# A two-layer convolution kernel on one core: a shorter transform step and an earlier input load in layer 0, and another order of the steps in layer 1

## The chip, the core and the metric

The kernel runs on one core of a Trainium2 chip. The core has five engines that work side by side, each through its own list of instructions in order: TensorE (PE, matrix products, its weight loads are listed as PEld), VectorE (DVE), ScalarE (ACT), GpSimd (POOL) and SyncE (SP), which here only issues DMA transfers. Engines wait for each other by semaphores. The metric is the device time of the whole program in microseconds (us), the median of several runs.

## The reference

The input `x` is 4 images of 64 channels, 256 by 256, in float32. Two layers follow each other, each on its group-normalised input, and each adds its result to its input:

```python
hidden = einsum('bchw,oc->bohw', x, w_hidden) + b_hidden          # 64 -> 384 channels
hidden = depthwise 3x3 convolution of hidden + b_dw
q, k, v = split(hidden, 3)                                        # 128 channels each
out = irfft2(rfft2(patches8x8(q)) * rfft2(patches8x8(k)))         # per 8x8 patch
out = layernorm over the channels of out * ln_w + ln_b
layer 0:  x = x + einsum('bchw,oc->bohw', v * out, w_proj) + b_proj

kern = w_span @ relu(batchnorm(w_reduce @ x)) + b_span            # 9 numbers per pixel
z = softplus(sum over the 9 taps of kern[tap] * x shifted by tap) # involution
layer 1:  x = x + softplus(conv3x3(z, w_conv2) + b_conv2)
```

## The kernel before, in words

**Stages.** A setup block makes the weights. A second block takes the statistics of the first image. Then comes layer 0, a short block that takes layer 1's statistics, and layer 1. Both layers walk over strips of 8 image rows: 128 strips in layer 0, 132 in layer 1 (the last few are padding). The order on each engine is written out by hand in functions called `body`; there is no scheduler. `run` (L411) and `run1` (L1187) call them: once plainly for the first pass and then in hardware loops.

**Layer 0.** One pass of `body` does two strips in eight steps, k = 0 to 7, four to a strip. `run` makes the plain first pass, and then, for each further image, a loop of 13 or 14 passes and a loop of one pass at the image's border, where the next image's statistics are finished (`averages` on PE, L622, while PE waits for DVE). The fourth and last long loop has 17 passes, i = 47 to 63. In a step PE makes four tiles of the q and k convolution (L550), in even steps `project` (L583, L585), in odd steps `variance` (L616, which needs the square `sq` that ACT makes at L719), the v convolution (L567), the forward transform (L606), and the inverse transform of the step before (L597, which needs `u` after POOL's subtraction of the mean, L517). ACT copies the results out of PSUM. After each forward transform `freq_copy` (L699) makes eight copies: two for `k_swap`, two for `q_im`, two for `q_re`, and two more of two partitions each (L711, L712), which put the purely real frequencies right. Once per strip ACT normalises the input, `normed` (L675, tile `xn`) in step 0, and rounds it, `high_parts` (L681) in step 1. POOL makes the low parts in step 2 (`low_parts`, L498); DVE adds up the results (`finish`, L852) and builds the stacked copies (`high_stacks`, `both_stacks`) behind it in steps 2 and 3, ahead of its product for step 3 (L818). SP loads the input (`load`, L429) for the strip after the one that was just normalised.

**Layer 1.** `body` does four strips. For a strip, PE spreads nine kernels over the channels (`select`, L1309, two banks in turn), DVE multiplies each with the shifted input (L1570, tile `prod`), and POOL adds seven of the nine products up (L1292, six additions), which DVE adds into `b_x` (L1518). ACT and DVE make the softplus and write `z` (L1528). PE convolves `z` in two halves of six products each (`conv`, L1327), DVE adds the input (`residual`, L1555), and POOL adds the logarithm (L1299) before the store. Besides, PE makes the next kernels: `r_product` (L1314) twice, ACT's relu between (L1443), then `weights` (L1319), split into three bfloat16 parts by ACT (L1451, L1456) and DVE (`rest` L1536, `third_parts` L1541), stored and read back in another layout by SP (`stack_parts`, `stack_back`). Bank 7 holds in turn the second half of the convolution, the relu's input, the kernels and the rest of the split, so these wait for each other.

Of the kernel before, what the change touches and what calls it, by code (L numbers as in the profile page):

```python
# [39 lines left out]
def build_program(nc, A, NI, S):  # L40
# [13 lines left out]
    with ExitStack() as ctx:  # L54
# [24 lines left out]
        imag_sign = sb("imag_sign", [P, 2])  # L79
        mean_w = sb("mean_w", [P, P])  # L80
# [10 lines left out]
        with ExitStack() as ph:  # L91
# [13 lines left out]
            wmax = tsb("wmax", [P, 4])  # L105
            loaded = ph.enter_context(nc.semaphore("weights_loaded"))
# [16 lines left out]
            def _(sp):  # L123
# [15 lines left out]
                sp.wait_ge(transforms_loaded, 16 * 24)  # L139
# [20 lines left out]
            def _(pool):  # L160
                for t in (bh, bdw, bd):
                    last = nc.gpsimd.memset(t[:, KQ:KV], 0.0)
# [7 lines left out]
            def _(v):  # L170
# [9 lines left out]
                v.wait_ge(v_loaded, 16 * 7)  # L180
                then(v.tensor_scalar(proj_scale[:], proj_w[:], ln_wb[:, 0:1], None, ALU.mult))
# [124 lines left out]
        with ExitStack() as ph:  # L306
# [60 lines left out]
            q_split = tsem("q_split")  # L367
# [43 lines left out]
            def run(eng, body, tail=None):  # L411
                body(0, True, NI > 1, None)
                start = 1
                for n in range(1, NI):
                    with eng.Fori(start, n * IT - 2) as i:
                        body(i, False, True, None)
                    with eng.Fori(n * IT - 2, n * IT - 1) as i:
                        body(i, False, n < NI - 1, n)
# [7 lines left out]
            def _(sp):  # L426
# [20 lines left out]
                def body(i, first, stats, image):  # L447
# [8 lines left out]
                    for b in range(2):  # L456
                        if not (first and b == 0):
                            to, of, of_res = i * 2 * R + b * R, i * 2 * R + (b + 1) * R, i * 2 * R + (b + 1) * R + 1
                            normed_before, pairs_before = i * 2 + b, i * 4 + 2 * b
                            if not first:  # L460
                                to, of, of_res = sp.snap(to), sp.snap(of), sp.snap(of_res)
                                normed_before, pairs_before = sp.snap(normed_before), sp.snap(pairs_before)

                            sp.wait_ge(xn_made, normed_before)
                            load(of, 1 - b)

# [19 lines left out]
            def _(pool):  # L486
# [33 lines left out]
                def body(i, first, stats, image):  # L520
# [21 lines left out]
            def _(pe):  # L542
# [83 lines left out]
                def body(i, first, stats, image):  # L626
                    for k in range(8):
# [5 lines left out]
                        for t in range(4):  # L633
                            if t % 2 == 0 and not (first and k == 0):
                                pe.wait_ge(qk_copied, i * 16 + (2 * k - 1 + t // 2))
                            last = conv(b, b_qk[t // 2][:, KQ * (t % 2):KQ * (t % 2) + KQ], 4 * cg + t)
                            if t % 2:
                                last.then_inc(qk_conv, 1)
# [9 lines left out]
                        def transform_ready():  # L648
                            pe.wait_ge(qk_copied, i * 16 + (2 * k + 2))
                            if not (first and k == 0):  # L650
                                pe.wait_ge(k_read, i * 8 + k)
                                pe.wait_ge(q_split, i * 8 + k)
# [15 lines left out]
            def _(act):  # L668
                def normed(s, b):
                    act.wait_ge(x_loaded[b], (s - b) * 16 + 32)  # L670
                    act.wait_ge(par_ready, s + 1)
                    if not isinstance(s, int) or s >= 1:
                        act.wait_ge(stacks_ready, s + 0)
                        act.wait_ge(hi_made, s + 0)
                    act.activation(xn[:, :, 0:SL], xr[b][:].rearrange("p s w -> p w s"), ACT.Identity, bias=par[b][:, 1:2],  # L675
                                   scale=par[b][:, 0:1]).then_inc(xn_made, 1)
# [21 lines left out]
                def freq_copy(i, k, any_before):  # L698
# [11 lines left out]
                    act.wait_ge(q_copied, i * 8 + k)  # L710
                    act.copy(by_block(q_re[C:C + 2, :]), b_q[C:C + 2])  # L711
# [1030 lines left out]
```

## Time and profile before

| what | value |
|---|---|
| median of 3 runs | 10036.34 us |
| lowest and highest | 10029.1 and 10041.79 us |
| the profiled execution's own time | 10034.93 us |
| its span, first to last instruction | 10033.1 us |
| mean granted clock of PE | 0.988 of full |
| busy: PE, DVE, ACT, POOL | 9128.4, 6036.7, 6973.9, 4896.1 us |

The profile is of one execution. The share of busy time is a mean over stages with different limits, so each stage is read by itself. Layer 0 runs from about 200 to 7110 us, layer 1 from about 7430 us to the end. In a row of the timeline, the number in square brackets is the time that the engine was idle just before, and the arrow names what ended it; "issue" means that no wait seen in the trace explains it.

### The profile page before, as it was taken

How to read it: one execution, taken by the hardware profiler on the slowest of the kernel's cores; microseconds unless marked ns; L12 is line 12 of the kernel's file. 1: busy time of each engine (PE TensorE's matmuls, PEld its weight loads, DVE VectorE, ACT ScalarE, POOL GpSimd, SP SyncE). 2: the span in 40 equal slices, each digit the busy share in tenths (PEclk: the TensorE clock that was granted, in tenths of full speed). 3: DMA queues.
4: the chain of work that ended last, by engine and by line, in shares of the span. 5: the costliest groups of instructions: out<-in, count | busy, mean ns of one | idle time of the engine just before them, and what ended most of it. 6: DMA issues, size and time to landing. Idle time of an engine off the chain costs nothing. (4 is left out here: it accounts for less than half of the span.)

```text
span 10033.1 us, 169594 instructions
## 1 busy us (share of the span) xinstructions
PE 9128.4 (91%) x58854; PEld 5045.6 (50%) x58854; DVE 6036.7 (60%) x7784; ACT 6973.9 (70%) x9573; POOL 4896.1 (49%) x2751
## 2 busy tenths in 40 slices
PE   1999999999999999999999999999868888888888
PEld 0666666666666666666665555555322222222222
DVE  4555555555555555555555454544558888888887
ACT  1777777777777777777776767767217777777777
POOL 1334433343344344433433333333118888888888
PEclk9999999999999999999999999999989999999999
DMA  6122222222222222222212111111764444444444
GB/s 129 47 60 55 48 57 56 56 50 55 60 55 47 59 56 55 50 55 60 55 39 48 39 48 39 47 40 39 162 157 105 104 104 104 104 104 104 104 104 102
DMA packets 619184, 718.26 MB, mean 72 GB/s; under 512 B 44324, under 2 KB 578138, under 8 KB 595142
## 3 DMA queue, kind: packets, MB, share of 16 engines
q1 hardware_dynamic: 618950, 714.70, 30.2%
q8 instruction: 200, 3.28, 0.1%
q14 instruction: 34, 0.28, 0.0%
HBM read 549.65 MB, written 164.89 MB: 71 GB/s over the span
## 5 line engine op out<-in xcount | busy, mean ns | idle before, releaser
L550 PE MATMUL banks<-w_hi,hi_lo 128*128 128x256 f16 x18432 | 2380.6, 275 | 132.5 <-issue 80.9
L550 PEld LDWEIGHTS banks<-w_hi,hi_lo 128*128 128x128 f16 x18432 | 1795.2, 99 | 556.4 <-issue 209.9
L508 POOL TENSOR_TENSOR u_im<-q_im,k_swap 128x512 f32<-128x512 f32 x512 | 706.4, 1380 | 2136.2 <-ACT q_im L706 2082.8
L1292 POOL TENSOR_TENSOR part_sum<-part_sum,prod 128x1024 f32<-128x1024 f32 x660 | 1559.8, 2363 | 261.7 <-DVE prod L1570 218.8
L1327 PE MATMUL banks<-z,conv_w 128*128 128x512 f32 x3140 | 1523.4, 614 | 0.0
L688 ACT ACTIVATE qk<-banks,inv_wscale 128x512 f32<-128x512 f32 x1024 | 689.9, 687 | 1040.8 <-PE banks L550 1028.4
L818 DVE TENSOR_TENSOR u<-q_re,banks 128x512 f32<-128x512 f32 x512 | 351.0, 686 | 1717.1 <-ACT q_re L712 1341.5
L511 POOL TENSOR_TENSOR u<-u,u_im 128x512 f32<-128x512 f32 x512 | 649.7, 1269 | 1338.8 <-DVE u L818 1338.8
L567 PE MATMUL banks<-hi_lo,w_hi 128*128 128x512 f16 x4608 | 1085.7, 381 | 13.9 <-DVE tmp L887 13.9
L550 PE MATMUL banks<-w_lo_pair,hi_pair 128*128 128x256 f16 x6144 | 1012.0, 274 | 0.0
L498 POOL TENSOR_TENSOR hl_all<-xn,hi_all 64x1280 f16<-64x1280 f32 x258 | 793.2, 3074 | 241.2 <-ACT hi_all L681 219.2
L1327 PEld LDWEIGHTS banks<-z,conv_w 128*128 128x128 f32 x3140 | 540.6, 188 | 613.2 <-issue 613.2
L517 POOL TENSOR_TENSOR u<-u,u_mean 128x512 f32<-128x512 f32 x512 | 532.2, 1039 | 513.4 <-DVE u_mean L833 513.4
L567 PEld LDWEIGHTS banks<-hi_lo,w_hi 128*128 128x128 f16 x4608 | 431.0, 98 | 650.5 <-issue 209.9
L597 PEld LDWEIGHTS banks<-idft,u 128*128 128x128 f32 x4096 | 496.3, 191 | 511.8 <-issue 322.7
L696 ACT ACTIVATE v_s<-banks,inv_wscale 128x512 f32<-128x512 f32 x512 | 349.6, 683 | 546.4 <-PE banks L567 546.4
L675 ACT ACTIVATE xn<-xr,par 128x2816 f32<-128x2816 f32 x129 | 684.0, 5302 | 27.0 <-DMA xr<-in_x_dram 27.0
L1570 DVE TENSOR_TENSOR prod<-banks,x_up 128x1024 f32<-128x1024 f32 x396 | 482.6, 1219 | 313.6 <-PE banks L1309 313.6
L597 PE MATMUL banks<-idft,u 128*128 128x128 f32 x4096 | 594.0, 288 | 73.8 <-POOL u L517 73.8
L550 PEld LDWEIGHTS banks<-w_lo_pair,hi_pair 128*128 128x128 f16 x6144 | 604.3, 98 | 72.6
L1309 PE MATMUL banks<-kern_parts,sel 64*128 64x512 bf16 x2380 | 443.7, 388 | 196.8 <-DVE prod L1570 196.5
L831 DVE TENSOR_REDUCE u_mean<-u 128x4 f32<-128x512 f32 x512 | 351.0, 686 | 434.0 <-POOL u L511 434.0
(210 smaller groups left out, 16400.3 us busy)
## 6 DMA issues: line engine op xcount, KB each, us to landing
xr<-in_x_dram SPq DMA_DIRECT2D x258, 640.0 KB, 9.1
xb<-y_scratch SPq DMA_DIRECT2D x268, 320.0 KB, 4.8
xa<-y_scratch SPq DMA_DIRECT2D x270, 256.0 KB, 5.3
x_res<-in_x_dram SPq DMA_DIRECT2D x258, 256.0 KB, 4.2
out_dram<-res SPq DMA_DIRECT2D x258, 256.0 KB, 5.1
y_scratch<-ys SPq DMA_DIRECT2D x256, 256.0 KB, 4.1
yc<-y_scratch SPq DMA_DIRECT2D x256, 256.0 KB, 6.0
xs<-in_x_dram SPq DMA_DIRECT2D x92, 512.0 KB, 7.1
```

Source lines behind the costliest of these rows:

```text
L498: nc.gpsimd.tensor_tensor(hl_all[C:P, 1 + c0:1 + c1, 1:SL], xn[C:P, c0:c1, 0:SL - 1], hi_all[C:P, 1 + c0:1 + c1, 0:SL - 1], ALU.subtract). ...
L508: nc.gpsimd.tensor_tensor(u_im[:], q_im[:], k_swap[:], ALU.mult).then_inc(u_made, 1)
L511: nc.gpsimd.tensor_tensor(u[:], u[:], u_im[:], ALU.add).then_inc(u_step, 1)
L517: nc.gpsimd.tensor_tensor(u4, u4, u_mean[:].unsqueeze(2).to_broadcast([P, 4, P]), ALU.subtract)\
L550: r = pe.matmul(out, px, w, start=n == 0, stop=n == 13)
L567: r = pe.matmul(b_v[:], w, px, start=n == 0, stop=n == 13)
L597: last = pe.matmul(by_patch[:, p, t], u[:, block], idft[:], start=True, stop=True)
L675: act.activation(xn[:, :, 0:SL], xr[b][:].rearrange("p s w -> p w s"), ACT.Identity, bias=par[b][:, 1:2], scale=par[b][:, 0:1]).then_inc(x ...
L688: act.activation(qk[:, 2 * h:2 * h + 2, :], b_qk[h][:].rearrange("p (t c) -> p t c", t=2), ACT.Copy, scale=inv_wscale[:, 0:1]).then_inc(qk ...
L1292: nc.gpsimd.tensor_tensor(part_sum[:], prod[0][:] if n == 0 else part_sum[:], prod[n + 1][:], ALU.add)\
L1327: last = pe.matmul(b_c[h][:], conv_w[:, n, :], z[b][:, 2 * h + j:2 * h + j + 2, dc:dc + W], start=n == 0, stop=n == 5)
L1570: v.tensor_tensor(by_row(to), by_row(flat(b_kern[(9 * k + n) % 2])), src[:, :, 1 + dc:1 + dc + W], ALU.mult).then_inc(prod_ready, 1)
```

## The change

**Layer 0.** The two small copies of `freq_copy` go, with their semaphore. In their place the setup block changes the transform's tables, so that the purely real frequencies pass through the same product as the others: the columns of `dft` become half the sum and half the difference of a pair, rows are added in `idft` (four more small loads, `idft_other`), and signs are changed. `normed` is done in two halves of the columns: the first in step 3 of the strip before, the second where the whole one stood, in step 0. SP loads a strip's input when the strip two before it has been normalised, ahead of the residual's load and the store. `averages` becomes eight small matmuls instead of one. The last pass, i = 63, has a loop of its own, so that the long last loop has 16 passes.

**Layer 1.** The same instructions stand in another order on every engine.

```diff
                     act.copy(by_block(q_re[0:C, :]), b_q[0:C])
                     act.copy(by_block(q_re[C:P, :]), b_q[0:C]).then_inc(q_copied, 1)
-                    act.wait_ge(q_copied, i * 8 + k)
-                    act.copy(by_block(q_re[C:C + 2, :]), b_q[C:C + 2])
-                    act.copy(by_block(q_re[C + 32:C + 34, :]), b_q[C + 32:C + 34]).then_inc(q_split, 1)
...
+                        if k % 4 == 3 and not (last and k == 7):
+                            normed(i * 2 + (k // 4 + 2), k // 4, 0)
                         if k % 4 == 0:
-                            normed(i * 2 + (k // 4 + 1), (k // 4 + 1) % 2)
+                            normed(i * 2 + (k // 4 + 1), (k // 4 + 1) % 2, 1)
...
                 def averages(image):
-                    pe.matmul(b_v[:, 0:2], pair_avg[:], tmp[:, 0:2, :].rearrange("p a i -> p (a i)"), start=True, stop=True)\
-                        .then_inc(gn_answered, 1)
+                    for q in range(4):
+                        for a in range(2):
+                            made = pe.matmul(b_v[32 * q:32 * q + 32, a:a + 1], pair_avg[:, 32 * q:32 * q + 32], tmp[:, a, :],
+                                             start=True, stop=True)
...
-                with eng.Fori(start, NB) as i:
-                    body(i, False, False, None)
+                with eng.Fori(start, NB - 1) as i:
+                    body(i, False, False, None, False)
+                with eng.Fori(NB - 1, NB) as i:
+                    body(i, False, False, None, True)
```

On POOL the last addition moves from the end of a strip to the start of the next:

```diff
+                        if not (first and k < 3):
+                            b = (k - 3) % 2
+                            nc.gpsimd.tensor_tensor(res[b][:], res[b][:], ab2[b][:], ALU.add).then_inc(out_ready, 1)
```

On SP, within a strip:

```diff
                         sp.wait_ge(mid_normed, normed_before)
-                        load_a(of_a, of_a1, (k + 1) % 2)
+                        load_a(of_a, of_a1, k % 2)
+                        stack_parts(made, k + 1)
                         if not (first and k < 3):
                             sp.wait_ge(out_ready, given_out)
                             store(to, (k + 1) % 2)
-                        stack_parts(made, k)
                         sp.wait_ge(parts_stored, stored)
-                        stack_back(0, (k + 2) % 4)
+                        for h in range(2):
+                            stack_back(h, (k + 1) % 4)
                         if not (first and k < 2):
                             sp.wait_ge(resid_added[1], given)
-                        stack_back(1, (k + 2) % 4)
                         load_b(of, (k + 2) % 4)
```

What stands in a row on the engines, at three places. The numbers behind `banks` are pairs of PSUM banks, those behind the other names are buffers.

ScalarE in layer 0, from the root of an odd step (step 3) into step 4, before:

```order
L726 ACTIVATE rs<-rs 128x512
L693 REGISTER_ALU
L696 ACTIVATE v_s3<-banks2,inv_wscale 128x512
L703 COPY k_swap<-banks1 64x512
L704 COPY k_swap<-banks1 64x512
L705 ACTIVATE q_im<-banks1,imag_sign 64x512
L706 ACTIVATE q_im<-banks1,imag_sign 64x512
L707 COPY q_re<-banks1 64x512
L708 COPY q_re<-banks1 64x512
L711 COPY q_re<-banks1 2x512
L712 COPY q_re<-banks1 2x512
L719 ACTIVATE sq0<-banks2 128x512
```

The same place in the changed kernel (the second half of `xn` follows two `qk` copies behind this piece):

```order
L703 ACTIVATE xn<-xr0,par0 128x128x11
L721 REGISTER_ALU
L724 ACTIVATE v_s3<-banks2,inv_wscale 128x512
L731 COPY k_swap<-banks1 64x512
L732 COPY k_swap<-banks1 64x512
L733 ACTIVATE q_im<-banks1,imag_sign 64x512
L734 ACTIVATE q_im<-banks1,imag_sign 64x512
L735 COPY q_re<-banks1 64x512
L736 COPY q_re<-banks1 64x512
L743 ACTIVATE sq0<-banks2 128x512
```

The first half of `xn` now stands before `v_s3`, and the two copies of two partitions before `sq0` are gone.

TensorE in layer 1, around the two products that make `r` (`x_mid` by `wr`), before:

```order
L1342 REGISTER_ALU
L1314 MATMUL banks3<-x_mid0,wr 128x512
L1337 REGISTER_ALU
L1309 MATMUL banks0<-kern_parts2,sel 128x512 x2
L1349 REGISTER_ALU
L1314 MATMUL banks3<-x_mid0,wr 128x512
L1337 REGISTER_ALU
L1309 MATMUL banks1<-kern_parts2,sel 128x512 x2
L1352 REGISTER_ALU
L1327 MATMUL banks3<-z1,conv_w 128x512
L1337 REGISTER_ALU
L1309 MATMUL banks0<-kern_parts2,sel 128x512 x2
```

The same in the changed kernel:

```order
L1378 REGISTER_ALU
L1340 MATMUL banks3<-x_mid0,wr 128x512
L1353 MATMUL banks3<-z1,conv_w 128x512
L1386 REGISTER_ALU
L1335 MATMUL banks1<-kern_parts3,sel 128x512 x2
L1389 REGISTER_ALU
L1340 MATMUL banks3<-x_mid0,wr 128x512
L1391 REGISTER_ALU
L1335 MATMUL banks0<-kern_parts3,sel 128x512 x2
L1353 MATMUL banks3<-z1,conv_w 128x512
L1395 REGISTER_ALU
L1345 MATMUL banks3<-rn,span_w 32x256 x4
```

The two products stood between the kernels of one strip (`kern_parts3`, or 2). Now they stand behind its last kernel, with a product of the convolution and a kernel of the next strip between them.

VectorE in layer 1, from the first product of a strip, before:

```order
L1564 REGISTER_ALU
L1568 REGISTER_ALU
L1570 TENSOR_TENSOR prod0<-banks0,x_up0 128x1024
L1573 REGISTER_ALU
L1574 REGISTER_ALU
L1518 TENSOR_TENSOR banks2<-banks2,part_sum 128x1024
L1564 REGISTER_ALU
L1570 TENSOR_TENSOR prod1<-banks1,x_up0 128x1024
L1551 REGISTER_ALU
L1553 ISA
L1554 ISA
L1555 SCALAR_TENSOR_TENSOR res0<-banks3,neg_b,xb0 128x512
```

The same in the changed kernel:

```order
L1610 TENSOR_TENSOR prod0<-banks1,x_up1 128x1024
L1602 REGISTER_ALU
L1610 TENSOR_TENSOR prod1<-banks0,x_up1 128x1024
L1556 TENSOR_TENSOR banks2<-banks2,prod8 128x1024
L1571 REGISTER_ALU
L1574 SCALAR_TENSOR_TENSOR banks3<-banks3,span_b,k_parts 128x256
L1618 REGISTER_ALU
L1619 REGISTER_ALU
L1556 TENSOR_TENSOR banks2<-banks2,part_sum 128x1024
L1579 TENSOR_TENSOR k_parts<-banks3,k_parts 128x256
```

The second product of the strip is now made first; the addition of `prod8`, which closed the strip before, comes behind it, and with it the two steps of the split (`span_b` and `k_parts`) of the next strip.

## Rows read from the trace of the kernel before

**Rows 1.** Stages: length; busy us of PE, PEld, DVE, ACT, POOL; clock; DMA:

```profile
200.00:5280.00 5080.00, 4923.42 (x38340) 3140.90 (x38340) 2768.92 (x3967) 3799.62 (x5176) 2006.56 (x1341) 1.00 0.23 54
5280.00:7110.00 1830.00, 1694.34 (x12868) 1068.10 (x12866) 891.24 (x1267) 1277.37 (x1744) 674.90 (x453) 0.97 0.18 42
...
7500.00:10033.00 2533.00, 2231.41 (x7062) 741.55 (x7060) 2074.24 (x2088) 1863.67 (x2611) 2160.08 (x915) 1.00 0.43 104
```

**Rows 2.** Waits over the whole run: us in total, times, longest us:

```profile
PE banks L616 <- ACT sq L719: 103.4, 128, 1.2
...
PE banks L550 <- issue: 80.9, 32, 3.3
...
PE banks L597 <- POOL u L517: 73.8, 127, 5.7
```

**Rows 3.** Timeline of ACT in layer 0: start us, us, what [idle before]:

```profile
3016.51 5.30 ACT L675 ACTIVATE xn<-xr,par 128x2816 f32<-128x2816 f32 x1
...
3037.34 0.58 ACT L711 COPY q_re<-banks 2x512 f32<-2x512 f32 x1
...
3057.75 0.69 ACT L696 ACTIVATE v_s<-banks,inv_wscale 128x512 f32<-128x512 f32 x1 [1.77 <-PE banks L567]
...
3069.09 5.32 ACT L675 ACTIVATE xn<-xr,par 128x2816 f32<-128x2816 f32 x1
```

**Rows 4.** Timeline of POOL and DVE in step 2 of a strip:

```profile
3042.81 2.71 POOL L498 TENSOR_TENSOR hl_all<-xn,hi_all 64x1280 f16<-64x1280 f32 x1
...
3042.99 3.52 DVE L852 TENSOR_TENSOR ys<-ys,t_n 128x512 f32<-128x512 f32 x1
```

**Rows 5.** Timeline of PE in the fourth long loop of layer 0:

```profile
5289.11 0.82 PE L550 MATMUL banks<-w_hi,hi_lo 128*128 128x256 f16 x3 [2.96 <-issue]
5291.74 1.44 PE L550 MATMUL banks<-w_hi,hi_lo 128*128 128x256 f16 x6 [1.81 <-issue]
...
5400.97 0.82 PE L550 MATMUL banks<-w_hi,hi_lo 128*128 128x256 f16 x3 [2.64 <-issue]
...
6978.48 0.82 PE L550 MATMUL banks<-w_hi,hi_lo 128*128 128x256 f16 x3 [3.27 <-issue]
```

**Rows 6.** DMA queue of instructions, 2800 to 3800 us, then 5600 to 6600 us:

```profile
q8 instruction: 13, 0.21, 0.1%
...
q8 instruction: 80, 1.31, 0.6%
```

**Rows 7.** Timeline of PE over one strip of layer 1:

```profile
8402.26 3.70 PE L1327 MATMUL banks<-z,conv_w 128*128 128x512 f32 x8
...
8409.94 0.39 PE L1309 MATMUL banks<-kern_parts,sel 64*128 64x512 bf16 x2 [1.20 <-DVE prod L1570]
8410.59 1.13 PE L1314 MATMUL banks<-x_mid,wr 128*128 128x512 f32 x2 [0.27 <-DVE res L1555]
...
8412.59 1.13 PE L1314 MATMUL banks<-x_mid,wr 128*128 128x512 f32 x2 [0.47 <-ACT rn L1443]
8413.99 0.39 PE L1309 MATMUL banks<-kern_parts,sel 64*128 64x512 bf16 x2 [0.27 <-DVE prod L1570]
8414.31 1.13 PE L1327 MATMUL banks<-z,conv_w 128*128 128x512 f32 x2
...
8421.59 3.70 PE L1327 MATMUL banks<-z,conv_w 128*128 128x512 f32 x8
```

**Rows 8.** Timeline of POOL over the same strip:

```profile
8420.34 2.36 POOL L1299 TENSOR_TENSOR res<-res,ab 128x1024 f32<-128x1024 f32 x1 [0.40 <-ACT ab L1470]
...
8427.13 12.13 POOL L1292 TENSOR_TENSOR part_sum<-part_sum,prod 128x1024 f32<-128x1024 f32 x5 [1.68 <-DVE prod L1570]
```

**Rows 9.** Page: a product on DVE (mean ns), loads to landing:

```profile
L1570 DVE TENSOR_TENSOR prod<-banks,x_up 128x1024 f32<-128x1024 f32 x396 | 482.6, 1219 | 313.6 <-PE banks L1309 313.6
...
xb<-y_scratch SPq DMA_DIRECT2D x268, 320.0 KB, 4.8
```

**Rows 10.** Timeline of the setup block: a small VectorE step, a small load's issue:

```profile
31.14 0.25 DVE L182 TENSOR_SCALAR proj_shift<-proj_w,ln_wb 128x64 f32<-128x64 f32 x1
...
14.69 0.47 SPq L134 DMA_DIRECT2D dft<-in_dft_dram  x1
```

More of the change, by code:

```diff
@@ L79, in build_program @@
         imag_sign = sb("imag_sign", [P, 2])
+        own_sign = sb("own_sign", [P, 1])
         mean_w = sb("mean_w", [P, P])
@@ L138, in _ @@
                                     .then_inc(transforms_loaded, 16)
-                sp.wait_ge(transforms_loaded, 16 * 24)
+                    sp.wait_ge(v_cleared, 1)
+                    for part in range(2):
+                        for half in range(2):
+                            lo, src = C * part + 32 * half, C * (1 - part) + 2 * half
+                            sp.dma_start(idft_other[lo:lo + 2], A["idft"][src:src + 2]).then_inc(transforms_loaded, 16)
+                sp.wait_ge(transforms_loaded, 16 * 28)
                 sp.wait_ge(turned, 16)
@@ L411, in run @@
             def run(eng, body, tail=None):
-                body(0, True, NI > 1, None)
+                body(0, True, NI > 1, None, False)
                 start = 1
@@ L445, in load_stats, with body @@
                                      A["x"][:, bass.ds(row + R * h, R), :]).then_inc(xs_loaded, 16)
-                def body(i, first, stats, image):
+                def body(i, first, stats, image, last):
                     if stats:
@@ L518, in less_mean, with body @@
                         .then_inc(u_ready, 1)
-                def body(i, first, stats, image):
+                def body(i, first, stats, image, last):
                     for k in range(8):
@@ L733, in next_root, with body @@
                     act.activation(g_root[:, 1:2], g_root[:, 0:1], ACT.Exp, scale=-0.5).then_inc(gn_answered, 1)
-                def body(i, first, stats, image):
+                def body(i, first, stats, image, last):
                     for k in range(8):
@@ L900, in next_params, with body @@
                                            src[:, 0:1, image:image + 1].to_broadcast([P, S, 1])))
-                def body(i, first, stats, image):
+                def body(i, first, stats, image, last):
                     for k in range(8):
@@ L1476, in body @@
                         u2, b2 = i * 4 + (k + 2), (k + 2) % 4
+                        v, bv = i * 4 + (k - 2), k % 2
+                        second_parts(u1)
+                        norm_up(u1, b1)
+                        if any_1:
+                            z_abs(i, k, any_2)
+                            z_exp(i, k)
+                        if any_2:
+                            conv_abs(v, bv, 0, not (first and k < 4))
+                        if any_1:
+                            z_log(i, k)
                         params(u2, b2)
@@ L1592, in _ @@
                 v.wait_ge(sel_ready, 2)
-                for u in range(2):
-                    rest(u)
-                    third_parts(u)
+                rest(0)
+                third_parts(0)
                 run1(v, body)
```

226 lines of the change are left out of this document (124 added, 102 removed).

## Prediction

> **What bounds the kernel now.** I read the stage table first [rows 1], then the waits of the whole run [rows 2], then one strip of each layer on the timeline. In the middle of layer 0 the reader is to see PE busy 4923 of 5080 us at full clock, while no other engine passes 3800: PE is the bound, and its 157 us of idle time are all that a better order can win there. The waits say who makes them: `variance` waits for ACT's square, 128 times and 103.4 us, and the inverse transform waits for POOL's `u`, 127 times and 73.8 us [rows 2]. That is one wait of each kind per strip, 1.38 us together. A third group, 80.9 us in 32 waits for "issue", has no releaser. All of it stands in the fourth long loop, where the clock is 0.97 as well [rows 1, 2]. In layer 1 a strip lasts 19.33 us [rows 7]; in 2533 us there are 131 of them, and per strip PE is busy 2231 / 131 = 17.0 us, POOL 16.5, DVE 15.8 and ACT 14.2 [rows 1]. Nobody is full: the engines hand over to each other one after another, and the order decides.
>
> **Layer 0, the two waits per strip: minus 177 us.** ACT's two copies of two partitions go, 0.58 us each [rows 3]: 1.16 per step, 4.6 per strip. Half of `xn` (2.65 of 5.3 us [rows 3]) leaves step 0 for step 3. The square that `variance` misses by about 0.81 us (103.4 / 128) is the one of step 1, behind `xn` of step 0: it now ends some 1.16 + 2.65 = 3.8 us earlier, so this wait goes. The other is `u` in step 3, missed by 0.58 us (73.8 / 127). DVE's product now waits for the first copies of `q_re` and not for the small ones, so `u` comes about 1.2 us earlier. PE, having lost its other wait, arrives 0.8 earlier too, measured from the strip's start, but so does all that feeds `u`; I lay it out with some 0.6 us to spare. It is the narrower of the two. The `finish` addition on DVE in that step still takes 3.52 us beside POOL's `low_parts` [rows 4], and the change leaves that as it was.
>
> The half of `xn` in step 3 stands before `v_s`, where ACT had 1.77 us idle [rows 3]. So `v_s` comes about 0.9 us later and the frequency copies about 0.6 us. PE wants them only in the next step, more than 3 us later, so this costs nothing; if that cover were gone it would be at most 0.9 us per strip, 115 us in all. The input load is issued a strip earlier in the queue and lands within 10 us, against 50 us until it is used: no cost. Waiting for both halves of `xn` delays the masks and `high_parts` by nothing, since the second half ends earlier than the whole did. Sum: 103.4 + 73.8 = 177 us. After that PE has no wait left in the strip, and it stands at about 52.58 - 1.4 = 51.2 us.
>
> **Layer 0, the fourth loop: minus 119 us.** At each of its 16 returns PE stands 2.96 us before the first matmul and 1.81 us before the fourth [rows 5]. The first pass starts at 5289.11 and the last at 6978.48, so a pass lasts 112.62 us, against 2 x 52.58 = 105.16 in the loops before [rows 3, 5]: 7.46 us each, of which 4.8 are standing and the rest is the lower clock after it. The instruction queue says why: 13 packets in a thousand us of the third loop, but 80 in a thousand of the fourth, nine per pass [rows 6]. A packet is 16,384 bytes (1.31 MB / 80), which holds 256 instructions of PE's compiled list, at 64 bytes each. The body has 1,656 instructions on PE, 6.5 packets. Counted in the compiled lists, the fourth loop begins about 9 instructions before the end of a packet's block, so that it touches eight blocks. The loops without a stall have 155, 192 and 229 instructions in their first block and touch seven. The change makes `averages` 28 instructions longer, three times ahead of the fourth loop, and this shifts it: the second to fourth loops now have 164, 173 and 182 in their first block, seven blocks each. I take the whole stall as gone, 16 x 7.46 = 119 us. No engine but PE has a body of more than a few blocks. The ends of this term are 0 and 119; the quiet loops are the nearest rows, so I take 119. The seven additional matmuls at each of three image borders are tiny ones in a wait for DVE that is there already: nothing.
>
> The Trainium skill ("Runtime: NRT & Kernel Launch", section "Instruction fetch mechanics") says that PE holds 2048 instructions, and also that a taken branch forces a fetch if its target lies outside a window of two pages. By the second, every return of every long loop would stall, before and after, and this term would be 0; this trace has 32 such waits in 16 of some 60 returns, so it does not agree with that rule, and it is nearer to the first.
>
> **Layer 1: minus 291 us.** A strip's four waits of PE are 1.20, 0.27, 0.47 and 0.27 us, 2.21 together [rows 7]. 19.33 - 2.21 = 17.12. The instructions are the same, so the floors stand: PE 17.0; POOL six additions of 2.43 (12.13 for five) and one of 2.36, 16.9 with hardly a gap [rows 8]. What keeps POOL from it now is a gap of 1.68 us before its second addition and 0.40 before the last [rows 8]; the order now puts the last addition at a strip's start and a product of DVE ahead of it, which fills both. I laid the new order out from these durations, with zero at a strip's first product on DVE: the old order comes to 19.2 in that layout, against 19.33. The narrow places of the new one: `third_parts` is ready at 6.2 us and PE wants bank 7 for the convolution at 6.4; the kernels' parts are back at about 13 and `select` of the next strip wants them at 16.5; `xb` lands at 20.5 (4.8 us of load [rows 9]) and is wanted at 21.4. All just hold. PE's larger number of changes between kinds of matmul (eight for seven) adds at most 0.3. I take 17.1: 131 x 2.22 = 291 us. The other ends: 16.9 by POOL (minus 26 us more), and 19.33, no gain.
>
> **Setup: plus 4.5 us.** Four loads at 0.47 us of issue and a dozen small VectorE steps at 0.25 [rows 10] make 4.9, of which a part lies beside other loads.
>
> **Sum.** 10033 - 177 - 119 - 291 + 4.5 = 9450. From start to start of the strips the first two waits come to 182 us in place of 177, since the clock and the gaps around them go too: 9446. The profiled execution took 1.8 us over its span and the median 1.4 more, so 9449 for the median.
>
> **Rivals.**
>
> *Layer 1 is held by another hand-over, at about 18 us.* Every margin above is below 1 us, and each is passed on through bank 7: relu, convolution, kernels, split. In the layout, 0.1 us more on each of ACT's instructions makes 17.7, and an `xb` that lands 3 us later makes 18.1. For it speaks that durations under load vary by such amounts (a DVE addition of 128x512 takes 3.52 us beside POOL, while a product of twice that size takes 1.22 in layer 1 [rows 4, 9]); against it, that DVE takes one operand from PSUM in nearly all of layer 1, and that the layout hits the old order. 131 x 0.85 = 111 us: 9560.
>
> *The stall at the loop's return stays or moves to another loop.* The counts could be off by a block, or a loop of seven blocks could stall too. Plus 119: 9568. The rule of two pages, named above, would come to the same.
>
> *A new wait takes the place of the four in layer 1*, and the strip stays at 19.3: plus 291, 9740.
>
> *The two waits of layer 0 stay*, because `u` depends on another step than I think: plus 177, 9626.
>
> *Slower than before, through SP.* In the new order the store of the output, which waits for POOL's last addition, stands in the queue ahead of the reading back of the kernels' parts. If POOL's addition comes late, the parts come late, `select` waits for them, and the next products and additions with it: a loop around the strip. It costs from the moment at which the parts land later than 16.5 us after the strip's start. To undo all gains a strip would have to reach 19.33 + 586 / 131 = 23.8 us, which needs the parts some 7 us later than that, at 23, where I have 13. POOL waits only for things that are long ready there, so I give it little.
>
> *The change does not do what it says:* the order on the engines shows that it does.
>
> **How the numbers follow.** All terms as taken, 9410 to 9490: 0.63. Layer 1 near 18: 0.17, 9560. The stall stays or moves: 0.09, 9568. Waits of layer 0 stay: 0.03. Layer 1 gains nothing, or several of these together: 0.06, 9620 to 9760. Slower: 0.02. The lower end is POOL's floor with a little more, 9400; the upper one takes in the second and third case with some of their spread, 9595. A measurement of this kernel can tell about 0.2%, 20 us, from no change; all cases but the last lie far on the faster side.
>
> **What would show it.** In layer 0 the waits of `variance` for the square and of the inverse for `u` should be gone, the strip 51.2 us and PE over 99% busy. The fourth loop should have no "issue" waits, the clock 1.00 throughout and some 13 instruction packets per thousand us. In layer 1 the strip should be 17.1 us, with PE's waits under 0.3 together and POOL over 95% busy. I am wrong if PE waits for bank 7 or for `kern_parts`, if a DVE addition under POOL grows, or if another loop shows packets at its return.

## The result and the profile after

The changed kernel takes 9389.71 us (median of 4 runs, 9387.43 to 9394.93), the kernel before 10036.5 us in the same runs. The ratio is 0.936, with an interval of 0.934 to 0.937. The forecast was 9449 us with a range from 9400 to 9595, so the time lies 10 us below the range and 59 us below the forecast. The direction came out as forecast, and the waits that were to go went; one step of the working for layer 1 and some sizes did not hold. The profiled execution has a span of 9385.9 us, 647.2 us less than before.

The stage table of the kernel after answers to [rows 1]. Its columns are the same: stretch, length, busy us of PE, PEld, DVE, ACT and POOL, clock, DMA.

```profile
2000.00:3000.00 1000.00, 1000.00 (x7820) 639.39 (x7818) 557.07 (x804) 693.90 (x918) 412.11 (x274) 1.00 0.24 57
5000.00:6000.00 1000.00, 999.50 (x7822) 639.73 (x7820) 535.26 (x767) 692.81 (x920) 412.35 (x275) 1.00 0.18 45
7500.00:8500.00 1000.00, 999.93 (x3201) 325.07 (x3199) 947.00 (x950) 832.29 (x1188) 976.79 (x415) 1.00 0.48 119
```

The first row is the middle of layer 0, the second its fourth long loop, the third layer 1. PE is busy all the time in each of them, and the clock is 1.00. POOL is busy 97.7% of layer 1, DVE 94.7%.

PE's waits over the whole run, which answer to [rows 2]: total us, times, longest.

```profile
PE banks L620 <- POOL u L540: 6.6, 4, 5.1
...
PE banks L639 <- ACT sq L743: 0.7, 1, 0.7
```

The wait for `u` has gone from 127 times to 4, the wait for the square from 128 times to one, and no wait for "issue" is left. The instruction queue moved 62 packets in the whole run, where it moved 80 within a thousand us of the fourth loop before [rows 6].

ScalarE's halves of `xn` in layer 0 (start us, us), which answer to [rows 3]:

```profile
3026.97 2.88 ACT L703 ACTIVATE xn<-xr,par 128x1408 f32<-128x1408 f32 x1
3039.61 2.84 ACT L703 ACTIVATE xn<-xr,par 128x1408 f32<-128x1408 f32 x1
3078.11 2.88 ACT L703 ACTIVATE xn<-xr,par 128x1408 f32<-128x1408 f32 x1
```

From the first row to the third a strip lasts 51.14 us, against 52.58. A half takes 2.86 us, so that two are 0.4 us longer than the whole was (5.30).

PE in layer 1, which answers to [rows 7], and POOL beside it, which answers to [rows 8]:

```profile
8399.61 1.10 PE L1340 MATMUL banks<-x_mid,wr 128*128 128x512 f32 x2
8400.55 1.02 PE L1353 MATMUL banks<-z,conv_w 128*128 128x512 f32 x2
8401.50 0.39 PE L1335 MATMUL banks<-kern_parts,sel 64*128 64x512 bf16 x2
8401.82 1.13 PE L1340 MATMUL banks<-x_mid,wr 128*128 128x512 f32 x2
8402.88 0.39 PE L1335 MATMUL banks<-kern_parts,sel 64*128 64x512 bf16 x2
...
8416.46 1.10 PE L1340 MATMUL banks<-x_mid,wr 128*128 128x512 f32 x2
```

```profile
8406.37 2.36 POOL L1317 TENSOR_TENSOR res<-res,ab 128x1024 f32<-128x1024 f32 x1
8408.70 2.36 POOL L1324 TENSOR_TENSOR part_sum<-prod 128x1024 f32<-128x1024 f32 x1
8411.14 12.13 POOL L1324 TENSOR_TENSOR part_sum<-part_sum,prod 128x1024 f32<-128x1024 f32 x5
8423.23 2.37 POOL L1317 TENSOR_TENSOR res<-res,ab 128x1024 f32<-128x1024 f32 x1
```

None of these rows has a bracket with idle time. PE's strip, from 8399.61 to 8416.46, lasts 16.85 us, and POOL's, from 8406.37 to 8423.23, 16.86.

Where the 647.2 us are, by the first and last matmuls of each stage in the two traces: the setup is 2.9 us longer; layer 0, from its first to its last q and k convolution, is 312.8 shorter (6866.5 to 6553.7); the block between the layers is 9.4 shorter; layer 1, from its first `r_product` to its last convolution, is 324.9 shorter (2575.5 to 2250.6); and the end is 3.0 shorter. The forecast had 301 for layer 0 (182 and 119), 291 for layer 1, and 0 for the rest but the setup.

### The profile page after: what moved, and what is told of

It is laid out like the page before. It is cut to its first block and busy times, and to the rows that moved or that the text cites. A ratio compares the mean times of both kernels' runs of the same rounds, so it can differ in the third digit from the quotient of the medians.

```text
span 9385.9 us, 168801 instructions
## 1 busy us (share of the span) xinstructions
PE 9042.0 (96%) x58884; PEld 5002.5 (53%) x58884; DVE 6029.8 (64%) x7793; ACT 6408.4 (68%) x8676; POOL 4911.1 (52%) x2751
## 5 line engine op out<-in xcount | busy, mean ns | idle before, releaser
L573 PE MATMUL banks<-w_hi,hi_lo 128*128 128x256 f16 x18432 | 2351.3, 273 | 51.7 <-DVE hi_lo L837 51.7
L531 POOL TENSOR_TENSOR u_im<-q_im,k_swap 128x512 f32<-128x512 f32 x512 | 727.3, 1421 | 2103.3 <-ACT q_im L734 2031.1
L1353 PE MATMUL banks<-z,conv_w 128*128 128x512 f32 x3128 | 1575.1, 619 | 0.0
L703 ACT ACTIVATE xn<-xr,par 128x1408 f32<-128x1408 f32 x258 | 737.4, 2858 | 33.7 <-DMA xr<-in_x_dram 26.9
L880 DVE TENSOR_TENSOR ys<-ys,t_n 128x512 f32<-128x512 f32 x256 | 585.8, 2288 | 8.7
L831 DVE COPY hl_all<-hi_all 64x2816 f16<-64x2816 f16 x129 | 124.1, 962 | 681.1 <-ACT hi_all L709 681.1
```

The costliest lines, as they stand in the source:

```text
L531: nc.gpsimd.tensor_tensor(u_im[:], q_im[:], k_swap[:], ALU.mult).then_inc(u_made, 1)
L573: r = pe.matmul(out, px, w, start=n == 0, stop=n == 13)
L703: act.activation(xn[:, cols, 0:SL], xr[b][:, :, cols].rearrange("p s w -> p w s"), ACT.Identity, bias=par[b][:, 1:2], scale=par[b][:, 0:1] ...
L880: v.tensor_tensor(out, out, t_n[:].rearrange("p (c r) -> p r c", r=R), ALU.add).then_inc(fin_step, 1)
L1353: last = pe.matmul(b_c[h][:], conv_w[:, n, :], z[b][:, 2 * h + j:2 * h + j + 2, dc:dc + W], start=n == 0, stop=n == 5)
```

## The experiments

The kernel before takes 10032 to 10037 us beside the experiments. A number that an experiment adds is measured against 9390 us, the changed kernel, or against the kernel before, as said.

### Each layer alone

*Layer 0 changed, layer 1 as before.*

> Layer 0 of the changed kernel with layer 1 of the kernel before. Both changes together saved 647 us of the span: 313 from the first to the last q and k convolution, 9 between the layers, 325 in layer 1, less 3 more in the setup. If the parts do not depend on each other, this kernel takes 10036.5 - 313 - 3 to 9 = about 9718 us. Rival: the saving of layer 1 rests on something of layer 0 (its code's place in the blocks of instructions); then the sum of the two single savings is not 647.

Measured: 9718.08 us, ratio 0.9685 (0.9669 to 0.9701), 313.8 us less than the kernel before beside it (10031.87).

*Layer 1 changed, layer 0 as before.*

> Layer 0 of the kernel before with the new order of layer 1: 10036.5 - 325 = about 9710 us, the strip of layer 1 16.85 us, and the fourth loop of layer 0 still with its waits at each return. If the two changes are independent, the two savings add up to 647.

Measured: 9708.08 us, ratio 0.9676 (0.9660 to 0.9692), 323.8 us less. Its trace has the three waits of layer 0 unchanged:

```profile
PE banks L616 <- ACT sq L719: 104.5, 128, 1.2
PE banks L550 <- issue: 80.0, 32, 3.2
PE banks L597 <- POOL u L517: 76.3, 127, 5.7
```

The two savings add up to 638 us against 647. The 9 us between them are about what the runs of one of these kernels scatter by (10029 to 10042 us for the kernel before). So the halves of the change are independent, and can be explained one by one.

### The fourth loop: where its code lies

*The kernel before, with four small matmuls repeated in the setup.*

```diff
                 pe.wait_ge(asked, 1)
+                for _ in range(4):
+                    pe.matmul(bank[0][:, 0:2], pair_avg[:], tmp[:, 0:2, :].rearrange("p a i -> p (a i)"), start=True, stop=True)
                 pe.matmul(bank[0][:, 0:2], pair_avg[:], tmp[:, 0:2, :].rearrange("p a i -> p (a i)"),
```

> The kernel before with four small matmuls more on PE ahead of layer 0, 16 instructions of PE. They shift the fourth loop by 16 places, from 9 to 249 instructions in its first block of 256; the other loops keep 138, 176 and 213. If the place in the blocks makes the stall, the 32 waits for issue and the lower clock go and the time is 10036.5 - 119 = about 9918 us. Rival: the stall belongs to the fourth loop itself, its 17 passes or its content: 10037 us, nothing changed.

Measured: 9918.72 us, ratio 0.9888 (0.9872 to 0.9905), 113 us less. The same stretch of the fourth loop that had 80 packets and a clock of 0.97 before reads, in this kernel:

```profile
5600.00:6600.00 1000.00, 974.99 (x7604) 621.70 (x7603) 522.36 (x742) 753.19 (x1026) 397.75 (x267) 1.00 0.19 45
```

There is no wait for "issue", and the clock is 1.00. In the traces layer 0 is 118 us shorter, and the instruction queue moves 56 packets in the whole run instead of 200, that is 16 times nine less. Nothing was changed but the place of the code, by 16 instructions. So the stall does not belong to the fourth loop's content. In the changed kernel, by the count of the compiled lists, the code is moved by the 84 instructions that `averages` has more ahead of this loop, and so some 113 us of its gain come from where its code lies.

*The changed kernel, with 18 and with 39 such matmuls (72 and 156 instructions).*

> The changed kernel with 18 small matmuls more ahead of layer 0, 72 instructions of PE. The four long loops then have 82, 92, 101 and 110 instructions in their first block, so that each touches eight blocks of instructions, where 154 to 182 touched seven. If eight blocks against seven is what decides, nine packets per pass are fetched in all four loops and each of some 57 returns costs up to 7.45 us: up to 9390 + 425 = 9815 us, less where the fetch is hidden behind the first 82 to 110 instructions. If only a border a few instructions behind the loop's start does it, 9394 us and no packets in the loops.

Measured: 9641.92 us (9628.95 to 9680.18), 252 us more. This is the only kernel here whose runs differ by half a per cent. Of the 252 us the small matmuls themselves take 9, in the setup block. Its profiled execution, of 9680 us, has 36 waits:

```profile
PE banks L575 <- issue: 206.9, 36, 7.9
```

They stand at all 12 returns of the first long loop (82 instructions in its first block), at all 14 of the second (92), but only at 10 of the 29 of the third and fourth (101 and 110). (The first long loop has 13 passes, the next two 15 and the last 16, so that there are 12, 14, 14 and 15 returns.) By the same count of the compiled list, a body of 1,656 instructions needs 120 of them in its first block to stay within seven blocks of 256. So it is the eight blocks that count, not a border close to the start. But eight blocks do not make every return stall: at 101 instructions 4 of 14 do, at 110 there are 6 of 15. Nor is anything fetched at the others: the instruction queue moves 387 packets against 62 in the changed kernel, nine for each of the 36 stalls and one more, and none at all from 4260 to 4660 us, in the third loop, where PE is busy for all of the 400 us. The expectation had the packets in every pass.

> The changed kernel with 39 small matmuls more ahead of layer 0, 156 instructions of PE: the first long loop then has 254 instructions in its first block, the second, third and fourth 7, 16 and 25. If a loop that touches eight blocks with its border near its start stalls at each return, as the fourth loop of the kernel before did, no packets in the first loop, nine per pass in the three others, and 14 + 14 + 15 = 43 returns at 7.46 us: 9390 + 321 + 8 for the padding = about 9720 us. Rival: the cost depends on which loop it is, or falls off as in the third and fourth loop of the kernel with 72 more: 9400 to 9600 us.

Measured: 9795.42 us, 406 us more, of which the small matmuls take 17 in the setup block. PE at two returns of the second loop and at two of the fourth (in brackets the idle time):

```profile
2219.20 0.61 PE L575 MATMUL banks<-w_hi,hi_lo 128*128 128x256 f16 x2 [6.40 <-issue]
2222.28 1.65 PE L575 MATMUL banks<-w_hi,hi_lo 128*128 128x256 f16 x7 [2.47 <-issue]
...
2332.77 0.61 PE L575 MATMUL banks<-w_hi,hi_lo 128*128 128x256 f16 x2 [6.70 <-issue]
...
6657.49 1.15 PE L575 MATMUL banks<-w_hi,hi_lo 128*128 128x256 f16 x9 [2.29 <-issue]
...
6766.91 1.16 PE L575 MATMUL banks<-w_hi,hi_lo 128*128 128x256 f16 x9 [2.39 <-issue]
```

All 43 returns of the three loops stall, each in two waits (86 in all), and none of the first loop's, as expected, with 450 packets. The sizes were not as expected: a pass of the second loop lasts 2332.77 - 2219.20 = 113.6 us, 11.3 more than 102.3, and one of the fourth 109.4, 7.1 more. The estimate had 7.46 for all. The second and third loops also load the next image's statistics and the fourth does not, so the fetches may meet more traffic there. That fits `after_pad72` too, where the stall's wait is 5.6 to 7.9 us in the first three loops and 3.2 to 3.7 in the fourth, but no run separates it from the place in the block.

### Layer 0: which edit removes which wait

*Both halves of `xn` together in step 0.*

```diff
-                        if k % 4 == 3 and not (last and k == 7):
-                            normed(i * 2 + (k // 4 + 2), k // 4, 0)
                         if k % 4 == 0:
+                            normed(i * 2 + (k // 4 + 1), (k // 4 + 1) % 2, 0)
                             normed(i * 2 + (k // 4 + 1), (k // 4 + 1) % 2, 1)
...
-                normed(1, 1, 0)
```

> The changed kernel with both halves of xn in step 0, one after the other (2.86 us each instead of 5.3 for the whole), the two small copies still gone. The removed copies alone bring the square of step 1 forward by 1.16 us, and it came 0.81 us late. If the copies carry the gain, the time is 9390 us, or up to 29 us more, since PE itself now comes 0.58 us earlier (0.23 us per strip left to wait). If the split of xn is what removes the wait for the square, it comes back whole: 9390 + 103 = about 9495 us. The wait for u stays gone in both.

Measured: 9393.99 us, ratio to before 0.9360 (0.9344 to 0.9376), not to be told from the changed kernel. The square behind `xn` is now ready just in time for `variance`. First the changed kernel, then this one:

```profile
3046.80 0.60 ACT L743 ACTIVATE sq<-banks 128x512 f32<-128x512 f32 x1
3050.16 1.08 PE L639 MATMUL banks<-sq,mean_w 128*64 128x512 f32 x4
```

```profile
3052.73 0.60 ACT L743 ACTIVATE sq<-banks 128x512 f32<-128x512 f32 x1
3053.40 1.08 PE L639 MATMUL banks<-sq,mean_w 128*64 128x512 f32 x4
```

With the split there are 2.76 us between the square's end and PE, without it 0.07.

*Two small copies back, `xn` in halves.* (`spare` is a tile that nobody reads.)

```diff
-                    act.copy(by_block(q_re[C:P, :]), b_q[0:C]).then_inc(q_copied, 1)
+                    act.copy(by_block(q_re[C:P, :]), b_q[0:C])
+                    act.copy(by_block(spare[C:C + 2, :]), b_q[0:2])
+                    act.copy(by_block(spare[C + 32:C + 34, :]), b_q[32:34]).then_inc(q_copied, 1)
```

> The changed kernel with two copies of two partitions put back at their old place in each frequency copy (into a tile that nobody reads), and the product on DVE waits for the second one, as before; xn stays in halves. The split moves the square of step 1 by 2.65 us, more than the 0.81 it was late, so its wait stays gone. The wait of the inverse transform for u, 0.58 us per strip, comes back: 9390 + 74 = 9464 us. Rival: that the half of xn taken out of step 0 also frees u: 9390 us. Rival: both waits return: 9570 us.

Measured: 9455.39 us, ratio to before 0.9422 (0.9406 to 0.9437), 66 us more than the changed kernel. Its waits:

```profile
PE banks L621 <- POOL u L541: 56.2, 125, 5.8
```

*Both undone, by the two edits above together.*

> The changed kernel with both edits of ScalarE undone together: xn whole in step 0 and two small copies back in each frequency copy. With the halves together alone the time stayed (9394 us), with the copies back alone it rose by 65 us to 9455. If the copies and the split each suffice to free the square, the wait for it returns only now: 9390 + 184 = about 9570 us. If the square's wait was removed by something else (the changed transform, the input load), it stays at about 9455 to 9460 us.

Measured: 9587.5 us, ratio to before 0.9553 (0.9537 to 0.9569), 198 us more. Its waits:

```profile
PE banks L640 <- ACT sq L746: 121.6, 128, 1.3
PE banks L621 <- POOL u L541: 58.6, 127, 5.8
```

The four kernels make a table: 9390 with both edits, 9394 with the copies gone alone, 9455 with the split alone, 9587 with neither. The copies hold `u`. Either edit frees the square. So in the kernel as it stands the split of `xn` buys no time that the removed copies had not bought, only the margin of 2.7 us. The move of the input load and the changed transform leave both waits in place, since in the last kernel they are there.

### Layer 1: what sets 16.85 us

*One product of the convolution left out.*

```diff
                         select(1, (k + 1) % 4, 9 * k + 10)
-                        if any_1:
-                            conv(1 - b, 0, (2,))
+                            pass
```

> The changed kernel without one of the twelve products of the convolution in each strip of layer 1 (product 2 of the first half; the output is not the reference's): PE has 0.47 to 0.6 us less per strip, 16.3 in place of 16.85. If PE alone sets layer 1, a strip becomes 16.3 us: 9390 - 131 x 0.5 = about 9325 us. If POOL, whose seven additions stand end to end over 16.86 us, is the bound as well, the strip stays at 16.85: 9390 us, and PE begins to wait for DVE's products.

Measured: 9391.77 us, no change. PE now waits once a strip, for ACT's relu and not for DVE's products as expected:

```profile
PE banks L1345 <- ACT rn L1475: 73.9, 134, 0.9
```

*POOL's last addition on half of the columns.*

```diff
-                            nc.gpsimd.tensor_tensor(res[b][:], res[b][:], ab2[b][:], ALU.add).then_inc(out_ready, 1)
+                            nc.gpsimd.tensor_tensor(res[b][:, 0:512], res[b][:, 0:512], ab2[b][:, 0:512], ALU.add).then_inc(out_ready, 1)
```

> The changed kernel with POOL's addition to the result on half of the columns in layer 1 (the output is not the reference's): POOL has 1.18 us less per strip. If PE sets the pace or both do, nothing changes, 9390 us, and POOL gets 1.2 us of idle time per strip. If POOL alone sets it, a strip comes down by up to 1.18 us: down to 9235 us, and PE is no longer without a wait.

Measured: 9390.03 us, no change. POOL now waits in every strip, where this entry was 4.2 us in 2 waits, and PE stays without a wait in the strips:

```profile
POOL part_sum L1324 <- DVE banks L1556: 135.5, 131, 2.7
```

*Both at once.*

> The changed kernel with both at once: one product of the convolution less on PE (about 0.55 us) and POOL's last addition on half of the columns (1.1 us) in each strip of layer 1 (the output is not the reference's). Each alone changed nothing. If PE and POOL both stand at the strip's 16.85 us and nothing else does, the strip now comes down to PE's 16.3 us: 9390 - 131 x 0.55 = about 9318 us. If a third chain (ACT's relu, bank 7) stands there as well, 9390 us.

Measured: 9331.39 us, ratio to before 0.9300 (0.9284 to 0.9315), 58 us less. Its strip, from one first `r_product` to the next, is 16.41 us:

```profile
8399.68 1.10 PE L1340 MATMUL banks<-x_mid,wr 128*128 128x512 f32 x2
...
8403.88 0.64 PE L1345 MATMUL banks<-rn,span_w 128*32 128x256 f32 x8 [0.55 <-ACT rn L1475]
...
8416.09 1.10 PE L1340 MATMUL banks<-x_mid,wr 128*128 128x512 f32 x2
```

Less work on PE alone or on POOL alone changes nothing, on both it does. PE and POOL are both the bound of the new order, each with 16.85 us of work in a row. The expectation had the left-out product at half its size: with both of its passes it takes 1.06 us of PE. Of these only 0.44 came back per strip, since this product stood between the second product by `wr` and `weights` and had covered ACT's relu there. The chain of work of the last kernel shows the relu on the critical path in its place (start us, us):

```profile
8401.96 1.07 PE banks L1340 x2
8403.03 0.02 issue
8403.05 0.79 ACT rn L1475
8403.84 0.04 issue
8403.88 0.64 PE banks L1345 x8
```

So 0.55 us of idle time and about 0.07 for the stop took the place of the 1.06. That is a look at how the new order works: this product of the convolution stands where ACT needs the time.

*The kernel before, with lighter work on DVE and POOL in layer 1.*

```diff
-                            nc.gpsimd.tensor_tensor(part_sum[:], prod[0][:] if n == 0 else part_sum[:], prod[n + 1][:], ALU.add)\
+                            nc.gpsimd.tensor_tensor(part_sum[:, 0:512], (prod[0] if n == 0 else part_sum)[:, 0:512], prod[n + 1][:, 0:512], ALU.add)\
...
-                    v.tensor_tensor(flat(b_x), flat(b_x), of[:], ALU.add).then_inc(x_step, 1)
+                    v.tensor_tensor(flat(b_x)[:, 0:512], flat(b_x)[:, 0:512], of[:, 0:512], ALU.add).then_inc(x_step, 1)
...
-                            v.tensor_tensor(by_row(to), by_row(flat(b_kern[(9 * k + n) % 2])), src[:, :, 1 + dc:1 + dc + W],
+                            r = 4 if n == 7 else 2
+                            v.tensor_tensor(by_row(to)[:, 0:r], by_row(flat(b_kern[(9 * k + n) % 2]))[:, 0:r], src[:, 0:r, 1 + dc:1 + dc + W],
```

> The kernel before, with eight of the nine products on DVE, the sums on DVE and the six additions on POOL on half of the columns in layer 1 (the output is not the reference's). PE's work is the same. PE's two waits for DVE's products, 1.47 us of a strip, should go. If a stop costs PE just the idle time that the trace shows, a strip becomes 19.33 - 1.47 = 17.86 us with the two other waits still there, 17.12 with none. If each stop also costs about 0.07 us of pipeline that is filled anew, it becomes 17.72 us with two stops, 16.83 with none. In both cases the whole kernel takes 10035 - 131 x 1.5 to 2.5 = 9710 to 9840 us.

Measured: 9925.47 us, ratio 0.9891 (0.9874 to 0.9907), only 111 us less where 195 to 325 were expected. PE, over part of a strip:

```profile
8406.58 0.60 PE L1309 MATMUL banks<-kern_parts,sel 64*128 64x512 bf16 x4
8407.85 0.39 PE L1309 MATMUL banks<-kern_parts,sel 64*128 64x512 bf16 x2 [0.67 <-DVE prod L1571]
8408.60 1.10 PE L1314 MATMUL banks<-x_mid,wr 128*128 128x512 f32 x2 [0.36 <-DVE res L1555]
8409.63 0.39 PE L1309 MATMUL banks<-kern_parts,sel 64*128 64x512 bf16 x2
8410.56 1.13 PE L1314 MATMUL banks<-x_mid,wr 128*128 128x512 f32 x2 [0.55 <-ACT rn L1443]
...
8427.11 1.10 PE L1314 MATMUL banks<-x_mid,wr 128*128 128x512 f32 x2 [0.36 <-DVE res L1555]
```

Three waits are left, 1.58 us in a strip of 18.51. DVE and POOL have far less to do and PE still stops three times, one of them for a product of DVE: their amount of work made the smaller part of the waits. ACT's work was left as it was here; but the changed kernel has all of the work on all engines and no stop, so what made the waits was the sequence. For PE's work alone the rows give 18.51 - 1.58 = 16.93 us, already less than the 17.12 that the idle times gave for the kernel before.

## Why the prediction was right or wrong

**What bounds the kernel.** Right for both layers: the waits named were the ones that went, and no other stage changed its length by more than 10 us.

**Layer 0, the two waits.** Right in direction and nearly in size. The strip went from 52.58 to 51.14 us, forecast 51.2. Over the layer the gain without the stall was 312.8 - 118 = 195 us, against 182. A pass of two strips went from 105.2 to 102.3 us, and 64 times 2.9 make 186. The other 8 are in the passes at the three image borders, which the working had at nothing: together they went from 341.1 to 324.1 us, which is 17 and not 9 less. PE waits there 3.3 us for DVE instead of 4.6, and this too comes from the removed copies, since it is 4.6 again in `copies_back`. Of the steps inside the term, "the product waits for the first copies, so `u` comes earlier" held (`copies_back`: 66 us, and 56.2 of waits). "3.8 us earlier" for the square was more than needed: without the split the square is still in time, with 0.07 us to spare (`xn_together`). The share of the split in the gain is zero.

**The fourth loop.** Right: 119 forecast, 113 measured by moving the code and nothing else (118 between the traces), and the packets and the low clock went with it. The rival in which the stall stays did not come about. The count of blocks held in four kernels, and `after_pad72` refined it: the stall sets in with the eighth block, but with 101 and 110 instructions in the first block only at some returns.

**Layer 1.** This is the step that failed. "19.33 - 2.21 = 17.12" took for PE's time without waits the strip less the idle time in brackets. The strip became 16.85, and 131 times the 0.27 us between are 35 of the 59 us missed. A stop costs more than its bracket. In the kernel before, the two `select` matmuls at 8409.94 last 0.39 us and the next begins 0.65 later, of which 0.27 is in the bracket: 0.38 is left [rows 7]. After, the same two begin at 8401.50 and the next matmul at 8401.82: 0.32. Four `select` matmuls in a row, first before, then after:

```profile
8408.13 0.61 PE L1309 MATMUL banks<-kern_parts,sel 64*128 64x512 bf16 x4
```

```profile
8412.29 0.61 PE L1335 MATMUL banks<-kern_parts,sel 64*128 64x512 bf16 x4
8412.82 1.99 PE L1353 MATMUL banks<-z,conv_w 128*128 128x512 f32 x4
```

Before, the next begins at 8409.94, 1.81 later with 1.20 in the bracket, so 0.61; after, 0.53. When PE runs on, the next matmul begins while the last is being finished; when it stops, that overlap is lost, and it counts as busy. Over all of layer 1 the median of a row that ends in a stop is 0.07 us above that of the same row without one: 0.39 and 0.32 for two `select` matmuls, 0.61 and 0.54 for four, 1.13 and 1.06 for a product by `wr`. Four stops a strip make 0.28.

Two smaller things nearly cancel. The strip of [rows 7] had a little less idle time than most: over 123 strips of that trace the mean is 2.28 us, which leaves 17.04 and not 17.12. Less 0.28 that would be 16.76, and the new order takes 16.85: it is dearer by 0.09 for PE, because its convolution comes in seven pieces in place of five, together 11.6 us of a strip against 11.3, and not all of that comes back in the other rows. The working had put at most 0.3 us on the new order's changes between kinds of matmul and left them out of the sum. `before_light`, still in the old order, agrees: its strips have a mean of 18.49 us with 1.54 of idle time, and 16.95 less three stops at 0.07 is 16.74.

The Trainium skill says so too ("TensorE: Matmul & The Clock Gate", section "Step-by-step: what each phase is for"): the draining of one matmul overlaps the filling of the next, so only an isolated one pays for it. The traces agree, with 0.07 us at each stop; they show when the matmuls begin, not what goes on in the engine.

The floors were mis-sized by the same error, as they came from busy time: "PE 17.0" was really 16.85, and "POOL 16.9" 16.86. That the gain would end where POOL's additions stand end to end was put down as the other end, 26 us below the forecast, which is 9423. The strip came down to that floor, and a little under the 16.9 that it was put at. The range's lower end, 9400, left 23 us under 9423 for everything else. Of the 60 us that the profiled execution lies below the forecast, layer 1 took 34, layer 0 took 12, and the setup, the block between the layers and the end 14. So 8 of the 10 us by which the range was missed are the floor of layer 1, put too high, and the rest is what stood at nothing elsewhere.

One sentence of this part was wrong on the mechanism: "the order now puts the last addition at a strip's start and a product of DVE ahead of it". POOL executes its additions in the same sequence before and after; only the place where the loop's body begins has moved in the code. Its gaps close because the products and the logarithm arrive earlier.

**The margins and the rivals of layer 1.** "Every margin is below 1 us" was right, and none of them was overdrawn: neither bank 7 nor `kern_parts` nor `xb` stops PE. SP's new order, the slower side, cost nothing that can be seen.

**The rest.** The block between the layers got 9.4 us shorter and the end 3.0, which the forecast had at zero: 12 of the 59 us. Of the first, 7.7 are PE's waits for the loads of `yc`, 34.1 us before and 26.4 after. The change does not touch that block. In the traces of the ten kernels here that have the changed layer 0 it lasts from 355 to 370 us (these waits are 33.0 in `less_pool`), in the four with the old one from 368 to 372. So a part of the 9.4 is luck of the execution, and what makes the rest isn't settled. The setup cost 2.9 us, forecast 4.5.

**Open.** Which single move within layer 1's order removes which of PE's four waits was not separated. Nor is the size of a stall at a loop's return explained, from 5 us in the fourth loop of `after_pad72` to 11 in the second of `after_pad156`, nor which returns stall when a loop touches eight blocks with more than 100 instructions in the first.

## What to carry to other kernels

When a wait of PE goes, it takes more than the idle time in its bracket: count 0.07 us more for each stop, and read the time without waits from a stretch where PE runs on, not from its busy time, and over many strips rather than one. Where a hardware loop is long, look at the instruction queue and at its returns before tuning its content: moving the code by 16 instructions was worth 113 us here, moving it by 156 the wrong way cost 406. When a change has two edits against the same wait, undo each alone; here one of them turned out to buy no time.

## What the runs showed of the hardware

A loop of 1,656 PE instructions runs without fetching anything as long as it touches seven blocks of 256. When it touches eight, its returns can stall, and each return that stalls fetches nine blocks. It then costs 5 to 11 us, as the mean of a loop: 3 to 9 us of standing, and a granted clock of half, 1.2 GHz, for 6.8 us around it in the kernel before and for 10.2 us in the third loop of `after_pad156`. With 7 to 92 instructions in the first block every return stalled; with 101 and 110 it was 10 of 29, nothing was fetched at the other 19, and the runs of that one kernel differed by 0.5%, where all the others stay within 0.2%. A stop of PE costs 0.07 us more than the idle time that the profile shows before the next matmul.
